# Products of probabilities and values: one key chunk in each of four slots, or two chunks in each of two

## The chip, the cores and the metric

One core of one Trainium2 chip runs the whole program in one launch. The metric is the device time of that core in microseconds. The engines are TensorE (PE, with its weight loads shown apart as PEld), VectorE (DVE), ScalarE (ACT), GpSimd (POOL) and SyncE (SP), which issues the DMAs.

## The reference

A pre-norm transformer layer in float32: batch B = 4, T = 512 tokens, width 512, 32 query heads of width 16 in 8 groups of four, each group sharing one key/value head, and a gated MLP of width 1376. What matters here is the attention in the middle:

```python
q = (x @ Wq) ...; k = (x @ Wk) ...; v = (x @ Wv) ...          # x = layernorm(resid)
q, k = q * cos + rotate_half(q) * sin, k * cos + rotate_half(k) * sin
att = einsum('bhgqd,bhkd->bhgqk', q, k) / sqrt(16), causal mask
probs = softmax(att)
ctx = einsum('bhgqk,bhkd->bhgqd', probs, v)
x = resid + ctx @ Wo;  x = x + mlp(layernorm(x))
```

## The kernel before, in words

The program has two phases, `phase_1` (projections, rotation, attention) and `phase_2` (output projection of all but the first batch, MLP). The change touches phase 1 alone.

Phase 1 runs over the 4 batches. A batch is 32 slots: 8 groups (`g`, one key/value head with its four query heads) by 4 slots (`i`). Each engine walks the same 32 slots with its own list of work (`iteration` of each engine), and semaphores keep them together. Batches 0 to 2 carry, besides their own attention, the preparation of the batch after them (`has_next`); the last batch carries the start of phase 2 (splitting Wo, the first output projection) instead.

In slot `i` of group `g` TensorE goes through four steps `j`. In each:

- `scores(b, g + 2, i, j)` (matmuls at lines 947 and 950) writes query-key scores of the group after next for one head into one of the three PSUM banks `ps_s`; four heads need four banks in slots 0 and 1 (512 and 384 keys wide) and two banks in slots 2 and 3. That is 12 banks for each group, numbered 0 to 11 here. A bank is written again only when VectorE has taken the row maximum of what was there three banks earlier (`row_max`, line 711). The maxima go, split into two parts and transposed by TensorE (line 956), through a DMA into the rows of the queries.
- `scores_t(b, g, i, j)` (line 972) writes the transposed scores, less the maximum, of key chunk `i` into one of three banks `ps_t`. ScalarE turns them into `probs` (line 585), GpSimd zeroes the masked triangle of the chunk (`mask_probs`, lines 517 and 519).
- `weighted_v(b, g, c)` (line 986) multiplies the probabilities of key chunk `c` (512, 384, 256 and 128 query columns for c = 0 to 3) by values that carry a column of ones, into `ps_o`. The four heads write 32 partitions each, and each product of float32 takes two passes, so a chunk is eight matmuls. It waits until GpSimd has masked the chunk. Chunk 0 also waits until ScalarE has copied out `ps_o` of the group before. The last one signals `pv_done`.
- `dense(...)` works at the next batch: units of four pieces in fixed slots (`UNIT_SLOT`): four transposes of x (slots 6, 7, 9, 10), five projections to be rotated (`R`, slots 11, 13, 15, 18, 22), the value projection (`V`, slot 17) and its transpose (`U`, slot 21). All use the one bank `ps_d`, so a unit waits until the unit before it has been read, by VectorE or ScalarE.

Where the products stand is given by `PV_LAG` and `PV_AFTER`: chunk 0 in slot 3 of its own group after step 2, chunk 1 in slot 0 of the next group after step 1, chunk 2 in slot 1 after step 0, chunk 3 in slot 2 after step 1. After the last group of the last batch chunks 1 to 3 follow in one row. ScalarE copies `ps_o` out in slot 2 (`o_evacuate`), before the exponentials of that slot, and SP then stores it (`store_o`).

VectorE in slot `i` takes the row maxima bank by bank, and after each bank one item of `next_work` or `batch_0_work`: for a rotated unit the slot after it holds `rope_cos` (line 694) and `rope_swap` (line 697), four slots after it `rotated_low` (line 702); for a transposed unit `xt_low` (line 683). GpSimd rotates (`rotate`, lines 501 and 503) in the slot after the unit, ahead of the mask of that slot.

Of the kernel before, what the change touches and what calls it, by code (L numbers as in the profile page):

```python
# [27 lines left out]
NKV, GROUP, DH = 8, 4, 16  # L28
F = 1376
TT, KC = T // P, D // P  # L30
# [23 lines left out]


MAX_AFTER = 3
PV_LAG, PV_AFTER = 3, (2, 1, 0, 1)
T_AFTER = 3
PIECE_AFTER = ((1, 1, 2, 3), (1, 3, 3, 3), (1, 1, 2, 3), (3, 3, 3, 3))
STATS_SLOT, MEAN_SLOT, APPLY_SLOT = 1, 3, 4  # L60
# [33 lines left out]
def positive(count):  # L94

    return not isinstance(count, int) or count > 0
# [117 lines left out]
def phase_1(nc, d, to):  # L214
    with ExitStack() as ctx:
# [117 lines left out]
        def _(sp):  # L333
            def load_x(b):
                for t in range(TT):
                    sp.dma_start(x_in[:, t], d["x"][b, P * t:P * (t + 1)]).then_inc(x_loaded[t], DMA)
# [88 lines left out]
            def iteration(b, has_next):  # L425
                if has_next:
                    sp.wait_ge(xn_ready, TT * (b + 1))
                    load_x(b + 1)
                unit0 = UNITS * b + PRE_UNITS
                number = UNIT_NO if has_next else LAST_NO  # L430
                for slot in range(TT * NKV):
                    g, i = slot // TT, slot % TT
                    if i == 0 and g + 3 < NKV:
                        stage_rows(b, g + 3, NKV * b + g + 3)
                    if i == 0 and g + 3 >= NKV and has_next:
                        stage_rows(b + 1, g + 3 - NKV, NKV * b + g + 3)
                    if i == 1 and (has_next or g < NKV - 1):
                        stage_max(g + 1, unit0 + number[slot - 1])
                    if i == PV_LAG - 1 and (g >= 1 or positive(b)):
                        store_o(b, g - 1)  # L440
                    if has_next and UNIT_SLOT.get(slot - LO_AFTER, "-")[0] == "R":
                        store_rotated(b + 1, UNIT_SLOT[slot - LO_AFTER][1])
                    if not positive(b) and i >= 2 and g < 6:
                        copy_raw(2 * g + i - 2)
                    if positive(b) and slot == SUMS_SLOT:
                        load_sums(b - 1)
                    if positive(b) and slot == INVERSE_SLOT + 1:
                        store_inverse(b - 1)
                    if not has_next:
                        prepare_batch_0(slot)  # L450
                if not has_next:
                    store_o(b, NKV - 1)
# [87 lines left out]
        def _(act):  # L540
# [63 lines left out]
            def iteration(b, has_next):  # L604
                unit0 = UNITS * b + PRE_UNITS
                slots, number = (UNIT_SLOT, UNIT_NO) if has_next else (LAST_SLOT, LAST_NO)
                for slot in range(TT * NKV):
                    g, i = slot // TT, slot % TT
# [6 lines left out]
                        v_evacuate(unit0 + number[slot - 1])  # L615
                    if i == 1 and (has_next or g < NKV - 1):
                        max_evacuate(b, g + 1, unit0 + number[slot - 1])
                    if i == PV_LAG - 1 and (g >= 1 or positive(b)):
                        o_evacuate(b, g - 1)
                        if g == 0:  # L620
                            v_place(b, unit0 - UNITS + V_NO)
# [6 lines left out]
                    if not has_next and WO_HI <= slot < WO_HI + KC:  # L628
                        c = slot - WO_HI
                        act.wait_ge(wo_loaded, DMA)  # L630
                        nc.scalar.copy(to.wo[0][:, c], to.wo[1][:, c].bitcast(F32)).then_inc(wo_hi_ready, 1)
                    if not has_next and FFN_HI <= slot < FFN_HI + KC:
                        c = slot - FFN_HI
# [239 lines left out]
        def _(pe):  # L873
# [118 lines left out]
            def iteration(b, has_next):  # L992
                unit0 = UNITS * b + PRE_UNITS
                slots, number = (UNIT_SLOT, UNIT_NO) if has_next else (LAST_SLOT, LAST_NO)
                for slot in range(TT * NKV):
                    g, i = slot // TT, slot % TT
                    kind, k = slots.get(slot, "--")
                    for j in range(GROUP):
                        if has_next or g < NKV - 2:
                            scores(b, g + 2, i, j)  # L1000
                        scores_t(b, g, i, j)
                        before, c = divmod(slot - PV_LAG, TT)
                        if j == PV_AFTER[c] and (before >= 0 or positive(b)):
                            weighted_v(b, before, c)
                        if i == 0 and j == MAX_AFTER and (has_next or g < NKV - 1):
                            transposed_max(NKV * b + g + 1, g + 1, unit0 + number[slot])
                        if kind == "T" and j == T_AFTER:
# [4 lines left out]
                                if PIECE_AFTER[i][piece] == j:  # L1012
                                    dense(b + 1, kind, k, unit0 + number[slot], piece)
                if not has_next:
                    for c in range(TT - PV_LAG, TT):
                        weighted_v(b, NKV - 1, c)

            pe.wait_ge(consts_ready, 1)
# [438 lines left out]
```

## Time and profile before

| | |
|---|---|
| time, median of 3 | 878.38 us (877.71 to 879.62) |
| the profiled execution's own time | 873.69 us |
| its span | 871.9 us |
| PE busy | 823.9 us, 94% |
| DVE, ACT, POOL busy | 54%, 38%, 20% |
| granted TensorE clock over the span | 0.99 |
| start, before the slots | 0 to about 68 us |
| batches 0, 1, 2, 3 of phase 1 | from about 68, 169, 269 and 369 us |
| phase 2 | from about 461 us |

A start in the timeline is in microseconds from the first instruction. The duration that stands with a matmul contains its way through the array, so that successive matmuls overlap; the distance from one start to the next is what it costs. One full-width matmul of 512 columns costs some 0.23 us so, and 0.39 us stand beside it.

### The profile page before, as it was taken

How to read it: one execution, taken by the hardware profiler on the slowest of the kernel's cores; microseconds unless marked ns; L12 is line 12 of the kernel's file. 1: busy time of each engine (PE TensorE's matmuls, PEld its weight loads, DVE VectorE, ACT ScalarE, POOL GpSimd, SP SyncE). 2: the span in 40 equal slices, each digit the busy share in tenths (PEclk: the TensorE clock that was granted, in tenths of full speed). 3: DMA queues.
4: the chain of work that ended last, by engine and by line, in shares of the span. 5: the costliest groups of instructions: out<-in, count | busy, mean ns of one | idle time of the engine just before them, and what ended most of it. 6: DMA issues, size and time to landing. Idle time of an engine off the chain costs nothing. (4 is left out here: it accounts for less than half of the span.)

```text
span 871.9 us, 13600 instructions
## 1 busy us (share of the span) xinstructions
PE 823.9 (94%) x4544; PEld 580.4 (67%) x4544; DVE 471.6 (54%) x861; ACT 332.4 (38%) x659; POOL 177.0 (20%) x349
## 2 busy tenths in 40 slices
PE   1869998999999999999999899999999999999998
PEld 1645665556555666556557688788887888888886
DVE  7569766797778785787753454333333233231112
ACT  2115544675466654675583222211112111121111
POOL 5213344333543253432330000000000000000000
PEclk9969999999999999999999999999999999999999
DMA  5166666631355224464518620041200411020001
GB/s 192 61 190 202 191 194 220 203 93 56 115 165 178 83 78 135 144 193 126 155 37 250 183 72 25 1 156 38 73 25 33 137 56 52 12 77 20 0 1 49
DMA packets 67824, 93.05 MB, mean 107 GB/s; under 512 B 7056, under 2 KB 34704, under 8 KB 67568
## 3 DMA queue, kind: packets, MB, share of 16 engines
q1 hardware_dynamic: 67776, 92.43, 34.1%
q8 instruction: 28, 0.46, 0.2%
q14 instruction: 20, 0.16, 0.1%
HBM read 60.16 MB, written 41.22 MB: 116 GB/s over the span
## 5 line engine op out<-in xcount | busy, mean ns | idle before, releaser
L711 DVE TENSOR_REDUCE m_raw<-ps_s 128x1 f32<-128x384 f32 (+3 forms) x384 | 215.5, 594 | 87.6 <-PE ps_s L950 86.5
L585 ACT ACTIVATE probs<-ps_t 128x512 f32<-128x512 f32 (+2 forms) x384 | 196.0, 529 | 125.3 <-PE ps_t L972 124.4
L947 PE MATMUL ps_s<-k_rows,q_rows 96*128 96x256 f32 (+3 forms) x512 | 166.5, 358 | 16.8 <-DMA k_rows<-scratch_k_parts 11.4
L972 PE MATMUL ps_t<-q_rows,k_rows 98*128 98x512 f32 (+2 forms) x384 | 167.0, 439 | 1.0 <-DMA q_rows<-m_t 0.8
L947 PEld LDWEIGHTS ps_s<-k_rows,q_rows 96*128 96x128 f32 x512 | 95.1, 194 | 89.5 <-issue 39.0
L1278 DVE TENSOR_TENSOR h<-h,bank 128x512 f32<-128x512 f32 (+1 forms) x44 | 30.2, 687 | 220.4 <-PE bank L1321 219.2
L950 PE MATMUL ps_s<-mask_q,ident_b 128*128 128x128 bf16 (+1 forms) x384 | 97.1, 253 | 0.0
L986 PE MATMUL ps_o<-probs,v_ones 128*32 128x512 f32 (+3 forms) x1024 | 95.2, 444 | 0.5 <-POOL probs L519 0.3
L1216 ACT ACTIVATE h<-bank 128x512 f32<-128x512 f32 (+1 forms) x44 | 26.3, 599 | 152.1 <-PE bank L1321 152.1
L519 POOL TENSOR_SCALAR_AFFINE_SELECT probs<-probs 128x512 f32<-128x512 f32 x128 | 81.4, 636 | 0.0
L972 PEld LDWEIGHTS ps_t<-q_rows,k_rows 98*128 98x128 f32 x384 | 76.8, 201 | 6.2 <-ACT probs L585 4.9
L1222 ACT CAST h_hi<-h 128x512 fp32r<-128x512 f32 (+1 forms) x44 | 27.3, 620 | 127.0 <-DVE h L1278 127.0
L950 PEld LDWEIGHTS ps_s<-mask_q,ident_b 128*128 128x128 bf16 x384 | 38.0, 99 | 48.8 <-issue 38.1
L517 POOL TENSOR_TENSOR carrier<-half 128x1 f32<-128x1 f32 x128 | 27.1, 212 | 212.2 <-ACT probs L585 212.2
L1373 PE MATMUL ps_y<-wd_hi,h_hi 128*128 128x512 f32 (+1 forms) x176 | 69.5, 395 | 0.0
L1373 PE MATMUL ps_y<-wd_hi,h_lo 128*128 128x512 f32 (+1 forms) x176 | 69.0, 392 | 0.0
L1373 PE MATMUL ps_y<-wd_lo,h_hi 128*128 128x512 f32 (+1 forms) x176 | 68.6, 390 | 0.0
L195 POOL TENSOR_TENSOR var_eps<-mean_var,eps 128x1 f32<-128x1 f32 x16 | 3.1, 191 | 289.5 <-DVE mean_var L190 289.5
L1321 PE MATMUL bank<-xt_hi,wu_hi 128*128 128x512 f32 (+1 forms) x128 | 50.6, 395 | 0.0
L1321 PE MATMUL bank<-xt_hi,wg_hi 128*128 128x512 f32 (+1 forms) x128 | 50.6, 395 | 0.0
L1321 PE MATMUL bank<-xt_hi,wu_lo 128*128 128x512 f32 (+1 forms) x128 | 50.5, 395 | 0.0
L1321 PE MATMUL bank<-xt_lo,wg_hi 128*128 128x512 f32 (+1 forms) x128 | 50.5, 394 | 0.0
(135 smaller groups left out, 1290.2 us busy)
## 6 DMA issues: line engine op xcount, KB each, us to landing
q_rows<-scratch_q_parts SPq DMA_DIRECT2D x64, 192.0 KB, 3.8
scratch_q_parts<-r_hi SPq DMA_DIRECT2D x32, 256.0 KB
scratch_o<-o_sb SPq DMA_DIRECT2D x31, 256.0 KB, 2.1
k_rows<-scratch_k_parts SPq DMA_DIRECT2D x64, 96.0 KB, 4.1
x_in<-in_x SPq DMA_DIRECT2D x16, 256.0 KB, 4.0
scratch_q_parts<-r_lo SPq DMA_DIRECT2D x16, 256.0 KB
x_res<-in_x SPq DMA_DIRECT2D x16, 256.0 KB, 2.8
o_in<-scratch_o SPq DMA_DIRECT2D x64, 64.0 KB
```

The source lines that it names most:

```text
L517: nc.gpsimd.tensor_tensor(carrier[:, g % 2, c:c + 1], half[:, 0:1], half[:, 0:1], ALU.add)
L519: nc.gpsimd.affine_select(out=diagonal, in_=diagonal, compare_op=ALU.is_ge, fill=0.0, base=0, pattern=[[0, GROUP], [1, P]], channel_multip ...
L585: nc.scalar.activation(probs[:, g % 2, heads * u:heads * (u + 1), CHUNK_AT[c]:CHUNK_AT[c + 1]], ps_t[:, (BANK_AT[c] + u) % S_BANKS, 0:head ...
L711: nc.vector.tensor_reduce(out=m_raw[:, g % 2, at:at + heads], op=ALU.max, axis=AXIS.X, in_=ps_s[:, (BANK_AT[i] + u) % S_BANKS, 0:heads * w ...
L947: nc.tensor.matmul(bank[:, place], q_rows[r][0:PAIR, j, P * q:P * (q + 1)].bitcast(F32R), k_rows[r][0:PAIR, 0:width].bitcast(F32R), start= ...
L950: nc.tensor.matmul(bank[:, :, P * q:width], ident_b[:], mask_q[:, 0:heads, :], start=False, stop=True).then_inc(scores_ready, 1)
L972: nc.tensor.matmul(ps_t[:, (BANK_AT[c] + u) % S_BANKS, 0:heads * width], k_rows[r][:, P * c:P * (c + 1)].bitcast(F32R), q_rows[r][:, heads ...
L986: mm = nc.tensor.matmul(ps_o[32 * j:32 * j + 2 * DH, P * c:T], v_ones[:, c, g % NKV, :], probs[:, g % 2, j, CHUNK_AT[c]:CHUNK_AT[c + 1]], ...
L1222: nc.scalar.copy(h_parts[0][0:m, r], h[0:m, r]).then_inc(h_hi_ready, 1)
L1278: nc.vector.tensor_tensor(h[0:m, r], h[0:m, r], bank[units["up", f] % BANKS][0:m, :], ALU.mult).then_inc(h_ready, 1)
L1321: mm = nc.tensor.matmul(out, weights(w, c), moving(m, c), start=(c == 0 and n == 0), stop=(c == chunks - 1 and n == 2))
L1373: mm = nc.tensor.matmul(ps_y[:, t], h_parts[w][0:m, r, P * t:P * (t + 1)], wd[p][0:m, f, :], start=(f == 0 and k == 0), stop=(f == FT - 1 ...
```

## The change

Chunks 0 and 1 of a group are multiplied together in slot 3 of the group after step 1, chunks 2 and 3 together in slot 1 of the next group after step 1. The slot in which ScalarE copies the result out and SP stores it stays 2 (`PV_EVACUATE` replaces `PV_LAG - 1`). After the last group chunks 2 and 3 follow, instead of 1 to 3. No matmul is added or removed, and no wait inside `weighted_v` is changed.

```diff
-PV_LAG, PV_AFTER = 3, (2, 1, 0, 1)
+PV_SLOT = {1: (-1, (2, 3), 1), 3: (0, (0, 1), 1)}
+PV_EVACUATE = 2
...
-                    if i == PV_LAG - 1 and (g >= 1 or positive(b)):
+                    if i == PV_EVACUATE and (g >= 1 or positive(b)):
                         store_o(b, g - 1)
...
-                    if i == PV_LAG - 1 and (g >= 1 or positive(b)):
+                    if i == PV_EVACUATE and (g >= 1 or positive(b)):
                         o_evacuate(b, g - 1)
...
                         scores_t(b, g, i, j)
-                        before, c = divmod(slot - PV_LAG, TT)
-                        if j == PV_AFTER[c] and (before >= 0 or positive(b)):
-                            weighted_v(b, before, c)
+                        after, chunks, at = PV_SLOT.get(i, (0, (), GROUP))
+                        if j == at and (g + after >= 0 or positive(b)):
+                            for c in chunks:
+                                weighted_v(b, g + after, c)
...
                 if not has_next:
-                    for c in range(TT - PV_LAG, TT):
+                    for c in PV_SLOT[1][1]:
                         weighted_v(b, NKV - 1, c)
```

## Rows read from the trace of the kernel before

**Rows 1.** The page, busy time of each engine: us, share of the span, instructions.
```profile
PE 823.9 (94%) x4544; PEld 580.4 (67%) x4544; DVE 471.6 (54%) x861; ACT 332.4 (38%) x659; POOL 177.0 (20%) x349
```

**Rows 2.** Windows, batches 1 and 3: busy us of each engine, clock, DMA share, GB/s.
```profile
169.00:269.00 100.00, 98.75 (x677) 58.88 (x676) 76.36 (x150) 59.32 (x124) 39.83 (x76) 1.00 0.41 121
...
369.00:460.00 91.00, 87.90 (x618) 49.40 (x617) 65.35 (x124) 61.13 (x130) 29.46 (x75) 1.00 0.41 123
```

**Rows 3.** Timeline of PE, batch 1, slots 12 and 13: start, us, instruction.
```profile
203.98 0.48 PE L972 MATMUL ps_t<-q_rows,k_rows 98*128 98x512 f32 x1
204.30 0.40 PE L947 MATMUL ps_s<-k_rows,q_rows 96*128 96x512 f32 x1
204.54 0.23 PE L950 MATMUL ps_s<-mask_q,ident_b 128*128 128x128 bf16 x1
204.59 0.48 PE L972 MATMUL ps_t<-q_rows,k_rows 98*128 98x512 f32 x1
205.00 0.85 PE L986 MATMUL ps_o<-probs,v_ones 128*32 128x384 f32 x8
205.78 0.50 PE L947 MATMUL ps_s<-k_rows,q_rows 96*128 96x512 f32 x1
206.12 0.23 PE L950 MATMUL ps_s<-mask_q,ident_b 128*128 128x128 bf16 x1
...
207.41 0.42 PE L972 MATMUL ps_t<-q_rows,k_rows 98*128 98x384 f32 x1
207.75 0.64 PE L986 MATMUL ps_o<-probs,v_ones 128*32 128x256 f32 x8
208.32 0.45 PE L947 MATMUL ps_s<-k_rows,q_rows 96*128 96x384 f32 x1
208.61 0.23 PE L950 MATMUL ps_s<-mask_q,ident_b 128*128 128x128 bf16 x1
```

**Rows 4.** Timeline of PE, end of phase 1, two narrow windows.
```profile
458.04 0.72 PE L986 MATMUL ps_o<-probs,v_ones 128*32 128x384 f32 x8
...
458.37 0.61 PE L986 MATMUL ps_o<-probs,v_ones 128*32 128x256 f32 x8
```

**Rows 5.** Timeline of DVE, batch 1, slot 12.
```profile
204.21 0.69 DVE L711 TENSOR_REDUCE m_raw<-ps_s 128x1 f32<-128x512 f32 x1 [2.32 <-PE ps_s L950]
204.82 0.68 DVE L694 TENSOR_TENSOR rot_c<-ps_d,cos 128x512 f32<-128x512 f32 x1
...
206.02 0.73 DVE L697 STREAM_SHUFFLE rot_s<-ps_d 128x512 f32<-128x512 f32 x1
206.65 0.67 DVE L711 TENSOR_REDUCE m_raw<-ps_s 128x1 f32<-128x512 f32 x1
```

**Rows 6.** Timelines of DVE and PE, batch 1, slots 19 and 20.
```profile
235.89 1.78 DVE L702 TENSOR_TENSOR r_lo<-rot_c,r_hi 128x512 fp32r<-128x512 f32 x1
...
238.32 0.51 PE L947 MATMUL ps_s<-k_rows,q_rows 96*128 96x512 f32 x1 [0.84 <-DVE m_raw L711]
```

**Rows 7.** Timelines of POOL and PE, batch 1, slots 23 and 25.
```profile
253.17 0.63 POOL L519 TENSOR_SCALAR_AFFINE_SELECT probs<-probs 128x512 f32<-128x512 f32 x1
...
253.76 0.45 PE L947 MATMUL ps_s<-k_rows,q_rows 96*128 96x384 f32 x1
```

**Rows 8.** Timelines of DVE and PE, batch 1, slot 10.
```profile
197.76 0.68 DVE L683 TENSOR_TENSOR xt_lo<-ps_d,xt_hi 128x512 fp32r<-128x512 f32 x1
...
198.02 0.47 PE L972 MATMUL ps_t<-q_rows,k_rows 98*128 98x512 f32 x1
198.50 0.33 PE L888 MATMUL ps_d<-ident,xn 128*128 128x128 f32 x1
```

**Rows 9.** Timelines of ACT and PE, batch 1, slot 22.
```profile
243.02 0.59 ACT L562 COPY v_next<-ps_d 128x512 f32<-128x512 f32 x1
...
243.66 0.50 PE L899 MATMUL ps_d<-xt_hi,w_hi 128*128 128x512 f32 x1 [0.29 <-ACT v_next L562]
```

**Rows 10.** Waits of PE from 70 to 450 us: total us, times, longest.
```profile
PE ps_s L947 <- DVE m_raw L711: 4.3, 6, 1.4
```

## The prediction, on record before the changed kernel ran

> **What bounds the kernel now.** I read the page first: TensorE is busy 824 of 872 us, every other engine at most 54% [rows 1]. Then the windows by batch: inside a middle batch TensorE has matmuls in flight for 98.75 of 100 us, VectorE for 76, and the clock is full [rows 2]; the reader is to see that phase 1 is bound by TensorE's stream, with VectorE as the only other engine that is near. The list of waits says how near: over some 380 us TensorE waited 4.3 us for VectorE to free a score bank, 6 times [rows 10]. Last the timelines of single slots, which give what a visit to the product of probabilities and values costs, and how much earlier than needed each bank, mask and copy was ready. That last quantity, which I call spare below, decides this case.
>
> **What joining two chunks saves.** Take chunk 1 in [rows 3]. Without a product between them, a transposed-score matmul is followed by the next score matmul after 204.30 - 203.98 = 0.32 us, and that by its mask after 0.24: 0.56. With the product in between the same stretch is 206.12 - 204.59 = 1.53. So the visit costs 0.97 us. Its stream alone: one pass of chunk 1 takes 0.33 us where a pass of chunk 2 follows it (its second pass starts at 458.04, the first pass of chunk 2 at 458.37 [rows 4]), so two passes take 0.65. The rest, 0.33, is the price of a visit: 0.09 on the way in, the remainder at the end and in the next score matmul, which stands with 0.50 instead of 0.40 us. Chunk 2: 208.61 - 207.41 = 1.20 with it; without it a 384-wide pair of distances is about 0.43, so 0.77, of which two thirds of chunk 1's stream, 0.43, and again 0.34. I take 0.33 for all four chunks. That nothing of it is left between two chunks in one row is what [rows 4] show: the second pass of chunk 1 and the first of chunk 2 are 0.33 apart, which is stream alone. The new kernel makes two visits for each group instead of four: 0.65 us less. There are 32 groups; the last had its chunks 1 to 3 in one row already. 31 x 0.65 = 20 us of TensorE time go. That is the upper end of what can be won.
>
> The Trainium skill, TensorEngine Tiling (Array Packing), Key Properties, states that a change of tiling mode drains TensorE; the 0.33 us above agree with a drain on both sides of a 32-column product. The same page, under PSUM Bottleneck, warns that a faster TensorE part may only move the bound to the engines that read PSUM; by that rule nothing of the 20 us need arrive, and the next part works out from rows how much does.
>
> **What the moved products uncover.** No product is gone; they are moved, and where one stood something else was hidden. Call the lead how much earlier than before TensorE reaches a point, counted from the start of the group. In slot 0 of a group the product of chunk 1 (0.97) is gone, in slot 1 the visit of chunk 2 (0.77) comes after bank 5 instead of before bank 5: at bank 5 the lead would be 1.74. Behind it stand chunks 2 and 3 together, then nothing in slot 2, chunks 0 and 1 together in slot 3: from bank 5 to the end of the group the new order is 1.74 - 0.65 = 1.09 us longer than the old. So a group ends at 1.09 minus the lead that it really had at bank 5. With the full lead it wins 0.65; with none it loses 1.09.
>
> The lead is capped by VectorE. Bank 5 needs bank 2 read. A bare reading is spaced at 0.60 us, and TensorE without a product needs 0.32 + 0.24 + 0.04 = 0.60 for each bank too, so any other work of VectorE in slots 0 and 1 shows. Group by group, for a batch with a next one:
>
> - Group 3: VectorE has the cosine product and the swap in slot 12. It works without a gap from 204.21 and ends bank 2 at 206.65 + 0.67 = 207.32 [rows 5]; TensorE started bank 5 at 208.32 [rows 3]. The spare is 1.00, so the lead is 1.00 and not 1.74: +0.1 us. That VectorE's chain here doesn't move with TensorE is seen from its having no gap.
> - Group 4 has the same two operations in slot 16: +0.1, and in slot 18 the projection behind the value unit loses its cover of chunk 3: a further 0.2 (my estimate: less than half of the next such place).
> - Group 5: VectorE's subtraction took 1.78 us instead of the 0.68 of its kind beside a rotation on GpSimd, and TensorE already waited for it at 238.32 [rows 6]. The lead at bank 3 is nil; only chunk 2's 0.77 remains at bank 5: +0.3. In slot 22 the projection waited for ScalarE's copy, ending 243.61, with chunk 3 (0.21 + 0.33 = 0.54) standing before it [rows 9]; chunk 3 is now earlier, the copy isn't: +0.55. Together +0.9.
> - Group 6: chunk 3 of group 5 is masked at 253.80, because two rotations stand before it on GpSimd. It was used in slot 26; now it is wanted in slot 25. TensorE began bank 5 at 253.76 [rows 7]; with a lead of about 1.35 (slot 23's swap delays VectorE a little) it begins at 252.4, and the joined product is due 0.65 later, at 253.05. It waits about 0.8: 1.09 - 1.35 + 0.8 = +0.5. While it waits, scores, transposed scores and the whole TensorE queue stand behind it.
> - Group 2: in slot 10 the transposes need the bank that VectorE empties at 198.44. They came at 198.50, and would have come at 198.02 + 0.32 = 198.34 [rows 8]. Without chunk 3 in front they would come at 197.80: 0.55 more wait. With 0.15 for the same operation in slot 8 the group wins nothing: +0.05.
> - Groups 0, 1 and 7 have spare: group 7 wins 0.6; group 0 0.3 (VectorE starts late over the turn of the loop, my estimate), group 1 0.4 (two normalisations in slot 4).
>
> Sum of a batch: -0.3 - 0.4 + 0.05 + 0.1 + 0.3 + 0.9 + 0.5 - 0.6 = +0.55; three batches +1.7. In the last batch VectorE is as busy (65 of 91 us) [rows 2], with the splitting of Wo and the first contexts in slots 4 to 20; five groups of the kind of group 3 at +0.1 to +0.5 give +1.5, groups 0 and 6 together win 0.6, and at the very end chunk 1's stream, 0.65, now stands before the last transposed scores, whose exponential, mask and product are the chain that closes the phase, and there is nothing else for it to hide behind; some 0.4 for chunk 3's cover in slots 26 and 28. Together +2.0. Sum: +3.7 us.
>
> The other edits cost nothing. ScalarE's copy of the result stays in slot 2 and no longer has to wait there; it is no engine that binds. SP's store follows the copy, so it comes no later. The copy must be done before chunk 0 in slot 3, which is only one step earlier. Chunk 1 is wanted a whole slot earlier than before, but its mask is made in slot 1 and it is used in slot 3. In the last group a wait of TensorE for the last mask is there in both. Phase 2 isn't touched.
>
> The profiled execution took 873.69 us; 873.7 + 3.7 = 877.4. The median of the runs shown is 4.7 above the profiled one, and I carry the difference over: 878.4 + 3.7 = 882.1 us.
>
> **Rivals.**
>
> A. *TensorE alone binds.* All of the 20 us arrive: 858 us. For it speaks the 98.75% in [rows 2]; against it the spare of 1.00 where 1.74 is needed, which is a fact of the rows. 5%.
>
> B. *VectorE's chain slides along (the other side).* The place is banks 2 to 5 of each group. If VectorE, idle for 2 us during the joined product of slot 3, starts each group with its earlier work done, then the caps of groups 0 to 5 shrink, and only the waits for mask, copy and transposes (0.8 + 0.55 + 0.2 + 0.55 = 2.1 a batch, 6.3 in all), group 5's old wait of 0.84 (2.5 in all) and about 2 us in the last batch remain: 20 - 11 = 9 us won, 869 us. It decides from the point where bank 5's real spare is over about 1.1 us in most groups. For it: VectorE sat idle 2.32 us before slot 12 [rows 5]. Against: it was idle there before, and the cap was there all the same. 18%.
>
> C. *The waits stack.* A late bank pushes the reading of the next, and the joined product of 1.9 us in slot 3 delays the swap, the rotation on GpSimd and the mask behind it. Then light groups lose too, 0.2 us more in each of 31: 888 us. 17%.
>
> D. *It comes out even*, the caps a little smaller than counted, within 0.2% of 878.4: 16%.
>
> My forecast, a small loss of 2 to 6 us: 44%.
>
> **How the numbers follow.** About 0.2%, 1.8 us, is what a measurement of this kernel tells from no change. Faster by more: A and B, 23%, and 2% for the mild side of D: 25%. Within: 17%. Slower: the forecast and nearly all of C, 58%. The range holds B and C and leaves A and the far ends out: 868 to 888 us. The forecast's own range is 880 to 885.
>
> **What would show it.** In the profile of the changed kernel the visits of L986 number 64 instead of 126, and the span between the two chunks of one visit holds no gap: this shows the saving. TensorE's waits for L711 should rise from 4.3 us to some 12, with bank 5 of groups 3 and 4 among them; a wait of about 0.8 us for the mask should stand at slot 25, of about 0.9 for the value copy at slot 22, and of about 0.7 for L683 at slot 10. If these waits are absent, B or A is right; if a light group (7) doesn't run about 0.6 us faster, the saving itself is wrong. If the batches take less than 98.5 us each, my caps are too hard.

## The result, and the profile after

The changed kernel is slower: 888.1 us, median of four (885.73 to 888.61), against 878.4 for the kernel before beside it; ratio 1.0107, interval 1.0087 to 1.0127. The direction was forecast, the size was not: +9.7 us where +3.7 were expected, just past the end of the range.

The page first: busy time of each engine, the granted clock in 40 slices, and the group of the products.

```profile
PE 822.1 (93%) x4544; PEld 592.2 (67%) x4544; DVE 467.8 (53%) x861; ACT 332.1 (37%) x659; POOL 177.0 (20%) x349
...
PEclk9967998999999999999999899999999999999999
...
L987 PE MATMUL ps_o<-probs,v_ones 128*32 128x512 f32 (+3 forms) x1024 | 85.5, 450 | 1.5 <-POOL probs L520 0.8
```

Every line number below is one higher than before from this change on (L986 is now L987, L711 is L712). The products went from 95.2 us in flight to 85.5 and TensorE's sum from 823.9 [rows 1] to 822.1, yet the span grew from 871.9 to 886.2. Next TensorE's waits, between 70 and 465 us (total, times, longest):

```profile
PE ps_s L948 <- DVE m_raw L712: 10.7, 14, 1.8
PE ps_d L957 <- DVE rot_s L698: 3.5, 6, 0.6
PE ps_d L889 <- DVE xt_lo L684: 2.9, 4, 1.2
PE ps_d L900 <- ACT v_next L563: 1.9, 3, 0.6
PE ps_t L973 <- ACT probs L586: 0.5, 1, 0.5
```

The first was 4.3 us [rows 10]; L889 and L900 were 0.5 and 0.9 in the kernel before, and the second, the transposed maximum that waits until VectorE has swapped halves out of `ps_d`, was not in the list of before and is not in the forecast either. The first four rows together hold 13.3 us more of waiting than before, against 20 us that the joining saves. By that alone the kernel would be faster.

The windows show what no list of waits does (columns as in [rows 2]; the clock is the number ahead of the last two):

```profile
147.00:245.80 98.80, 93.27 (x651) 58.96 (x650) 73.60 (x146) 57.43 (x120) 39.24 (x74) 1.00 0.44 133
245.90:249.20 3.30, 3.30 (x24) 1.74 (x23) 1.30 (x4) 1.12 (x4) 0.78 (x2) 0.50 0.63 191
249.40:348.20 98.80, 93.18 (x650) 58.75 (x648) 73.29 (x146) 57.64 (x120) 38.49 (x73) 1.00 0.39 116
348.30:351.60 3.30, 3.30 (x21) 1.76 (x23) 2.29 (x4) 1.72 (x4) 1.41 (x4) 0.50 0.54 131
```

Once in each middle batch, in group 5, the granted clock is 0.50, that is 1.2 instead of 2.4 GHz, for some 3.4 us. In batch 0 the same place has it for 6.7 us, from 140.1. What stood before it is in TensorE's timeline of slots 19 and 20 (start, duration, operation):

```profile
238.59 1.71 PE L987 MATMUL ps_o<-probs,v_ones 128*32 128x512 f32 x16
240.23 0.44 PE L948 MATMUL ps_s<-k_rows,q_rows 96*128 96x128 f32 x2
...
244.52 0.50 PE L948 MATMUL ps_s<-k_rows,q_rows 96*128 96x512 f32 x1 [1.81 <-DVE m_raw L712]
...
246.78 1.51 PE L987 MATMUL ps_o<-probs,v_ones 128*32 128x256 f32 x16
```

The same joined product of chunks 2 and 3 took 0.86 us at full clock (in group 7, at 271.37), here 1.51. VectorE in that stretch:

```profile
241.19 0.73 DVE L698 STREAM_SHUFFLE rot_s<-ps_d 128x512 f32<-128x512 f32 x1
242.10 1.76 DVE L703 TENSOR_TENSOR r_lo<-rot_c,r_hi 128x512 fp32r<-128x512 f32 x1
```

Lastly the lengths of the groups, from the start of one group's first transposed scores to that of the next, batch 1, worked out from the timelines (batch 2 agrees within 0.02 us in both kernels, but for group 0 of the changed one, which takes 9.77 there):

```
group       0      1      2      3      4      5      6      7
before    9.98  11.32  13.72  15.39  15.46  14.59   9.89   9.89
after     9.46  11.67  13.83  15.57  15.99  16.97  10.13   9.28
           -0.52  +0.35  +0.11  +0.18  +0.53  +2.37  +0.24  -0.60   (from unrounded starts)
forecast   -0.3   -0.4  +0.05   +0.1   +0.3   +0.9   +0.5   -0.6
```

### The profile page after: what moved, and what is told of

Its sections match the earlier page's. It is cut to its first block and busy times, and to the rows that moved or that the text cites. A ratio compares the mean times of both kernels' runs of the same rounds, so it can differ in the third digit from the quotient of the medians.

```text
span 886.2 us, 13600 instructions
## 1 busy us (share of the span) xinstructions
PE 822.1 (93%) x4544; PEld 592.2 (67%) x4544; DVE 467.8 (53%) x861; ACT 332.1 (37%) x659; POOL 177.0 (20%) x349
## 5 line engine op out<-in xcount | busy, mean ns | idle before, releaser
L712 DVE TENSOR_REDUCE m_raw<-ps_s 128x1 f32<-128x384 f32 (+3 forms) x384 | 214.1, 594 | 107.7 <-PE ps_s L951 106.2
L948 PE MATMUL ps_s<-k_rows,q_rows 96*128 96x256 f32 (+3 forms) x512 | 161.4, 357 | 21.7 <-DVE m_raw L712 10.7
L973 PE MATMUL ps_t<-q_rows,k_rows 98*128 98x512 f32 (+2 forms) x384 | 171.6, 451 | 3.2 <-DMA q_rows<-m_t 2.6
L948 PEld LDWEIGHTS ps_s<-k_rows,q_rows 96*128 96x128 f32 x512 | 97.9, 200 | 59.9 <-DVE m_raw L712 24.7
L951 PE MATMUL ps_s<-mask_q,ident_b 128*128 128x128 bf16 (+1 forms) x384 | 98.9, 258 | 0.0
L987 PE MATMUL ps_o<-probs,v_ones 128*32 128x512 f32 (+3 forms) x1024 | 85.5, 450 | 1.5 <-POOL probs L520 0.8
L973 PEld LDWEIGHTS ps_t<-q_rows,k_rows 98*128 98x128 f32 x384 | 79.6, 208 | 7.5 <-ACT probs L586 3.7
L987 PEld LDWEIGHTS ps_o<-probs,v_ones 128*32 128x32 f32 x1024 | 27.3, 112 | 39.3 <-issue 23.8
```

What stands on the lines that cost most here:

```text
L712: nc.vector.tensor_reduce(out=m_raw[:, g % 2, at:at + heads], op=ALU.max, axis=AXIS.X, in_=ps_s[:, (BANK_AT[i] + u) % S_BANKS, 0:heads * w ...
L948: nc.tensor.matmul(bank[:, place], q_rows[r][0:PAIR, j, P * q:P * (q + 1)].bitcast(F32R), k_rows[r][0:PAIR, 0:width].bitcast(F32R), start= ...
L951: nc.tensor.matmul(bank[:, :, P * q:width], ident_b[:], mask_q[:, 0:heads, :], start=False, stop=True).then_inc(scores_ready, 1)
L973: nc.tensor.matmul(ps_t[:, (BANK_AT[c] + u) % S_BANKS, 0:heads * width], k_rows[r][:, P * c:P * (c + 1)].bitcast(F32R), q_rows[r][:, heads ...
L987: mm = nc.tensor.matmul(ps_o[32 * j:32 * j + 2 * DH, P * c:T], v_ones[:, c, g % NKV, :], probs[:, g % 2, j, CHUNK_AT[c]:CHUNK_AT[c + 1]], ...
```

## The experiments

Three theories. **T1, the caps:** the joining saves its 0.65 a group and the readers of PSUM on VectorE and ScalarE take it back, as forecast. **T2, the clock:** a wait behind which the granted clock falls costs more than its own length. **T3, the order:** it is not the joining but which chunk is moved out of which slot.

**The kernel before, once more** (`r_before`, unchanged).

> The kernel before once more, for a second profile of it. Its first profile took 873.7 us at a mean clock of 0.990, while 17 other executions of it stood at 0.970 to 0.978 and 876.6 to 882.5 us. Theory: the first profile was an execution in which the clock stayed full at the start of the slots; this one shows 876 to 880 us, with group 0 of batch 0 some 4 to 5 us longer at half clock and all groups of batches 1 and 2 as in the first. Rival: the 5 us lie elsewhere, in the middle groups or the second phase.

879.08 us, ratio 0.9996. Its profile is not like the first one of before:

```profile
44.00:78.00 34.00, 29.15 (x107) 19.34 (x107) 24.53 (x49) 9.06 (x18) 3.93 (x9) 0.50 0.68 212
78.20:463.00 384.80, 375.62 (x2579) 221.56 (x2576) 284.61 (x548) 232.06 (x487) 145.27 (x293) 1.00 0.45 137
```

Here the clock is 1.2 GHz for the 34 us in which the slots begin, and group 0 of batch 0 takes 13.08 us; in the first profiled execution it is full from 60.6 us and that group takes 8.38. This is not the whole difference of the two profiles: the slots begin 2.4 us earlier in the second, group 1 of batch 0 is 0.9 shorter, and phase 2 is 2.6 longer, with two more stretches at half clock, one of them this:

```profile
463.80:467.10 3.30, 3.30 (x9) 2.52 (x9) 1.19 (x2) 0.66 (x2) 0.00 (x0) 0.50 0.77 248
```

Together the span is 4.0 us longer. Batches 1 and 2 agree group by group within 0.01 us, and the clock there is full. So this profile (span 875.9) is the one to compare with: after is 10.3 longer, 8.3 of it in phase 1 (404.91 against 396.63), 1.35 ahead of the slots, 0.7 in phase 2. Of the 8.3, group 5 of three batches is 7.6 (2.88, 2.37, 2.38). In batch 0 that group took 15.57 before and not 14.60, because TensorE also waited 0.71 us there for the DMA of `k_rows`, which it doesn't in the changed kernel.

**Which join** (T3). Chunks 0 and 1 joined and the others alone; chunks 2 and 3 joined and the others where they were. (The chunks that follow after the last group are adapted in each of these kernels; the cuts leave that line out.)

```diff
 # e1_join01
+PV_SLOT = {1: (-1, (2,), 0), 2: (-1, (3,), 1), 3: (0, (0, 1), 1)}
 # e2_join23
+PV_SLOT = {0: (-1, (1,), 1), 1: (-1, (2, 3), 1), 3: (0, (0,), 2)}
```

> Half of the change: chunks 0 and 1 together in slot 3, chunks 2 and 3 left where they were. Theory 1 (covers and clock): one visit less for each group is worth 0.33 us, 10 us in all; chunk 1 no longer covers slot 0, so the wait of TensorE for VectorE in slot 20 grows from 1.0 to about 2.0 us in each of three batches, as in the changed kernel, and the granted clock falls to half behind it for some 3.4 us; the waits at slot 10, 22 and 25 don't appear. Sum -10 + 3 (slot 20) + 3 (other capped groups) + 4 (clock) = about 878 us, 874 to 884. Rival (only the covers count, the clock falls for reasons of its own): 874 us and the same stretches at half clock as in the changed kernel's first group. Rival 2 (a visit costs nothing to join): slower than before by the waits alone, 884 or more.

> The other half: chunks 2 and 3 together in slot 1, chunks 0 and 1 left where they were. Theory 1: -10 us for the visits; slot 20's wait stays at 1.0 us because chunk 1 still covers slot 0, so the clock doesn't fall in the middle batches; the waits at slot 10 (0.7), slot 22 (0.9) and a small one at slot 25 appear, +1.5 us a batch. About 873 us, 869 to 878. Rival (the clock falls wherever waits add up, also from slots 10, 22 and 25): 880 us or more with half-clock stretches in groups 5 and 6.

`e1_join01` 892.5 us, 1.0137 (1.0099 to 1.0175): a miss of 14 us. It has the loss of the change and more: group 5 takes 18.0 to 19.5 us with 7 to 10 us at half clock, groups 3 and 4 lose 0.5 each. `e2_join23` 876.2 us, 0.9973 (0.9951 to 0.9995): group 5 takes 14.78, the clock doesn't fall in the middle batches, the light groups win 0.3 to 0.4. So the join of chunks 2 and 3 alone is slightly good, by 0.27%, and inside the 869 to 878 expected. The loss came with the other, which takes chunk 1's product out of slot 0, from before the bank that VectorE frees late.

**Both pairs joined, but a slot later** (T3): chunk 1 back in slot 0, with chunk 0.

```diff
 # e3_later
+PV_SLOT = {0: (-1, (0, 1), 1), 2: (-1, (2, 3), 1)}
+PV_EVACUATE = 3
```

> The same joining, but the pairs stand later instead of earlier: chunks 0 and 1 together in slot 0 of the next group after step 1, chunks 2 and 3 together in slot 2 after step 1, result copied out in slot 3. So slots 0 and 2 keep their cover. Theory 1: all of the 0.65 us for each group arrive, the wait in slot 20 shrinks to nothing, no wait at slots 10, 22, 25, clock full: 856 to 864 us. Rival (VectorE's total work caps phase 1 wherever the products stand): no more than 5 us below before, 873 or more. Rival 2 (a long product burst by itself makes the score banks or the exponentials late): waits of TensorE for VectorE or ScalarE above 10 us, 875 us or more.

886.3 us, 1.0080 (1.0054 to 1.0105): a miss. Where it was aimed it hit, group 5 is 0.74 shorter than before and group 6 0.62 in batch 1, with a full clock there. The gain went elsewhere. TensorE's waits, same columns and stretch as above:

```profile
PE ps_s L948 <- DMA k_rows<-scratch_k_parts: 3.6, 3, 2.6
PE ps_s L948 <- DVE m_raw L712: 3.4, 10, 0.5
PE ps_d L889 <- DVE xt_lo L684: 3.2, 4, 1.2
PE ps_d L900 <- DVE xt_lo L684: 2.1, 3, 0.7
PE ps_t L973 <- DMA q_rows<-m_t: 1.9, 2, 1.6
```

Group 1 lost 0.88, and in the last batch the last two groups lost 3.5 (four chunks now stand at the tail) and the first two 1.6 against the first profile of before, 1.0 against the second. So this order uncovers other things; which product had covered which was not taken apart.

**Is it the subtraction?** VectorE's L703 stands before bank 3 of group 5 and took 1.76 us. In one kernel it works on one column of 512 for that unit, in the other zeros are written in its place; neither computes the low part of that unit.

```diff
 # e4_no_low2
+                width = 1 if k == 2 else T
-                nc.vector.tensor_tensor(r_lo[:, r], rot_c[:, r], r_hi[:, r].bitcast(F32),
+                nc.vector.tensor_tensor(r_lo[:, r, 0:width], rot_c[:, r, 0:width], ...
 # e5_zero2
+                if k == 2:
+                    nc.vector.memset(r_lo[:, r].bitcast(F32), 0.0).then_inc(r_lo_ready, 1)
+                    return
```

> The changed kernel with one piece of VectorE's work left out: the subtraction of rotated unit 2, in slot 19, is done on 1 column instead of 512 (the low part of those queries is then not computed). Theory 1: the wait of 1.8 us in slot 20 falls to about 0.3, and as that wait is what lets the clock fall in group 5, the half-clock stretches of batches 1 and 2 go too: three times 1.6 + 1.4 = 9 us less than the changed kernel's 888, 879 us, group 5 of batch 1 about 14 us instead of 16.97. Rival (the clock falls for reasons of its own, with the start of the run): only three times 1.6, 883 us, group 5 at 15.4 us with the clock still halved there.

> The changed kernel, with the subtraction of rotated unit 2 in slot 19 replaced by writing zeros (the low part of those queries is left out). One column of that subtraction still took 1.23 us in e4, because it stood behind GpSimd's rotation, which reads two tensors; a write of zeros reads nothing. Theory 1 (the lock with GpSimd makes the wait of slot 20, and that wait lets the clock fall): zeros take about 0.5 us and don't wait for GpSimd; TensorE's wait in slot 20 falls from 1.8 to under 0.8, the half-clock stretches of batches 1 and 2 in group 5 are gone, group 5 takes 14.3 to 14.8 us instead of 16.97, and the median is 6 to 8 us below the changed kernel's 888: 880 to 882. Rival (the waits of slots 21, 22 and 25 are enough to make it fall): group 5 still above 16 us, 883 to 885. Rival 2 (no lock; VectorE is late because of its own amount of work): zeros take over 1 us as well, nothing moves.

`e4_no_low2`: 889.0 us, no better, and the miss is the finding. (Its profiled execution took 880.0; group 0 of batch 0, 9.03 us there and about 13 in most profiles, holds some 4 of the 9.) Timelines of VectorE, GpSimd and TensorE:

```profile
235.35 1.23 DVE L704 TENSOR_TENSOR r_lo<-rot_c,r_hi 128x1 fp32r<-128x1 f32 x1
...
235.25 1.31 POOL L502 TENSOR_TENSOR rot_s<-rot_s,sin 128x512 f32<-128x512 f32 x1 [2.97 <-DVE rot_s L698]
...
237.24 0.49 PE L949 MATMUL ps_s<-k_rows,q_rows 96*128 96x512 f32 x1 [1.28 <-DVE m_raw L713]
```

One column took 1.23 us and ended at 236.58, when the first half of GpSimd's rotation had ended (236.56). So most of it isn't work. The rotation is a product (L502) and a sum (L504), each of two tensors in SBUF. The wait of 1.28 us that is left again stands before a stretch at half clock:

```profile
238.90:242.20 3.30, 3.30 (x24) 1.62 (x24) 1.54 (x4) 0.94 (x3) 0.68 (x2) 0.50 0.60 181
```

`e5_zero2`: a write with no input isn't held. VectorE's row, and the window over the place that fell in the others:

```profile
242.54 0.48 DVE L704 MEMSET r_lo<- 128x512 f32 x1
```
```profile
240.00:249.00 9.00, 7.87 (x61) 4.67 (x53) 6.80 (x16) 5.60 (x13) 4.85 (x8) 1.00 0.32 82
```

TensorE's wait is 0.62, the clock is full in group 5, which takes 14.48, 14.25 and 14.28 us, as expected; the time is 881.5, 1.0024 (0.9993 to 1.0055). Against 16.97 that is 2.7 us for each middle batch, of which 1.2 is the shorter wait (1.81 to 0.62). The other 1.5 goes with the stretch of 3.3 us at half clock; `q_after`, below, gives the same price inside one kernel. The Trainium skill, SBUF — State Buffer, Who interferes with whom, states that a VectorE operation with two SBUF inputs and a GpSimd operation that reads SBUF block one another whole; the 1.23 us for a single column agree.

**Half of the change by order, the other half without its block** (T3). Chunks 2 and 3 joined in slot 2; then the same place cured by turning two items of VectorE, so that the subtraction runs at the head of its slot, ahead of GpSimd's rotation, in both kernels and in both good variants.

```diff
 # e6_join23_late
+PV_SLOT = {0: (-1, (1,), 1), 2: (-1, (2, 3), 1), 3: (0, (0,), 2)}
 # f_before, f_after, f_join23 (on e2), f_e6 (on e6): the turned item
-                    work.append(lambda: rotated_low(b + 1, split))
+                    work.insert(0, lambda: rotated_low(b + 1, split))
```

> Chunks 0 and 1 where they were before, chunks 2 and 3 together in slot 2 after step 1, where chunk 3 was. Slot 2 keeps its cover, slot 0 too; only slot 1 loses chunk 2's. Theory 1: the wait for x low at slot 10, for ScalarE's copy at slot 22 and for the mask at slot 25 are as before or smaller, the lead at bank 5 is 0.77 where the spare was 1.0, so all of the 0.33 us for each of 31 groups arrives: 10 us less, 867 to 871, no half clock in the middle batches. Rival (bank 5 or the transposed maximum is capped as soon as any cover leaves): 875 to 878.

> The changed kernel with one item of VectorE's order turned: in a slot that holds the subtraction of a rotated unit and the cosine product and swap of another (slot 19), the subtraction comes first, before GpSimd can start its rotation. Everything is computed. Theory 1 (lock with GpSimd, then the wait of slot 20, then the clock): the subtraction takes 0.7 us instead of 1.8, the wait of slot 20 falls under 1 us, group 5 takes 14.3 to 15 us instead of 16.97 with the clock full, and the median is about 882 us, as with the zeros (881.5). Rival (the subtraction now waits for ScalarE's high part, or the later swap delays the rotation and the masks as much as was won): group 5 above 16 us, 886 or more.

> The kernel before with the same turned item. The wait of 0.84 to 1.0 us in slot 20 goes in three batches: 3 us less, about 876 us, clock no different. Rival: nothing, because the wait is covered by chunk 1 standing before it.

> Chunks 2 and 3 together in slot 1 (e2, 876.2 us), with the same turned item. If both gains are independent: 876.2 - 3 = 873 us, better than the kernel before, the changed one and e2. Rival: the wait for ScalarE's copy in slot 22 or the mask in slot 25 takes it back, 876.

> Chunks 2 and 3 together in slot 2 (e6, 879.3), with the turned item. Group 5 without the wait of slot 20. If the two add up: 876; if e6's loss lay in a late VectorE in the last batch, which the turned item doesn't touch, the same 876, and then the joining in slot 1 (f_join23, 874.2) stays the better one. Below 873 would say that covers in slot 2 are worth more than the one in slot 1.

```
kernel           us      ratio (interval)           group 5, batch 1
e6_join23_late   879.3   1.0017 (0.9991 - 1.0042)   14.02
f_after          885.7   1.0062 (1.0028 - 1.0095)    14.96
f_before         875.0   0.9945 (0.9918 - 0.9972)    13.51
f_join23         874.2   0.9947 (0.9929 - 0.9964)    14.27
f_e6             873.5   0.9948 (0.9917 - 0.9978)    12.93
```

Turned, the subtraction takes its own time and TensorE's wait at that bank shrinks (rows of VectorE and TensorE, `f_after`):

```profile
239.60 0.68 DVE L703 TENSOR_TENSOR r_lo<-rot_c,r_hi 128x512 fp32r<-128x512 f32 x1
...
244.11 0.50 PE L948 MATMUL ps_s<-k_rows,q_rows 96*128 96x512 f32 x1 [0.73 <-DVE m_raw L712]
```

Group 5 of the changed kernel falls from 16.97 to 14.96, with a full clock there. But `f_after` (about 882 expected, a miss) has falls elsewhere. One is in group 1 of batch 1, right after two short waits for row maxima:

```profile
184.64 0.45 PE L948 MATMUL ps_s<-k_rows,q_rows 96*128 96x384 f32 x1 [0.70 <-DVE m_raw L712]
185.70 0.44 PE L948 MATMUL ps_s<-k_rows,q_rows 96*128 96x384 f32 x1 [0.31 <-DVE m_raw L712]
...
186.10:192.80 6.70, 6.70 (x37) 4.55 (x36) 4.48 (x9) 2.98 (x6) 0.78 (x2) 0.50 0.10 37
```

It costs 3.1 us (group 1 takes 14.75 us there and 11.66 in batch 2); a second one of 3.4 us, in group 3 of the last batch, costs 1.5. `e5_zero2` has the first one too, from 186; the changed kernel itself, with the same waits, does not. Turning helps the kernel before (-4 us of median, 3 expected) at least as much as the changed one, so the block is an old loss that the change enlarged, not the whole of its loss: `f_after` stays 10.7 us above `f_before`. `e6_join23_late` (867 to 871 expected, a miss) wins 1.5 us in each middle batch and gives 2.1 back in the last, where TensorE waits 2.3 for VectorE; turned, it has the lowest median of the kernels that compute everything, but its interval and those of the other two lie on one another. The wait of 2.3 us bears on T2, for the clock did not fall behind it:

```profile
425.13 0.51 PE L948 MATMUL ps_s<-k_rows,q_rows 96*128 96x256 f32 x2 [2.34 <-DVE m_raw L712]
...
425.10:435.00 9.90, 9.49 (x69) 5.34 (x70) 9.58 (x19) 7.11 (x15) 3.04 (x8) 1.00 0.12 41
```

**The caps** (T1). In the pair `q_before` and `q_after` each row maximum is taken over the first 64 keys of a bank only, and the exponential is scaled by a thousandth so that no sum runs over: VectorE's readings are short, everything else keeps its place. In `n_after`, built on `f_after`, the normalisation of batches 1 to 3 works on 8 of 512 columns, which frees VectorE in slots 4 and 5.

```diff
 # q_before, q_after
-                        ACT.Exp, scale=SCALE).then_inc(exp_done, 1)
+                        ACT.Exp, scale=SCALE * 1e-3).then_inc(exp_done, 1)
...
-                        in_=ps_s[...].rearrange("p (j t) -> p j t", j=heads)
+                        in_=ps_s[...].rearrange("p (j t) -> p j t", j=heads)[:, :, 0:64]
 # n_after
+                width = D if isinstance(b, int) and b == 0 else 8
+                nc.vector.tensor_scalar(xn[:, t, 0:width], x_in[:, t, 0:width], ...
```

> The kernel before, with the row maximum taken over the first 64 keys of each bank only, so that VectorE's reading of a bank is short (some 0.2 us instead of 0.6), and the exponent scaled by 0.001 so that the exponentials stay finite; probabilities are not the reference's. It is the base for the next one. Theory: TensorE's waits for VectorE (4.3 us) mostly go: 870 to 876.

> The changed kernel with the same short row maximum. Theory 1 (the cap by VectorE's reading eats the saving): with the cap gone the groups with a short chain win their 0.65 us against q_before; groups 5 and 6 still pay for the value copy, the mask and the locked subtraction. Group 3 and 4 turn from +0.2 and +0.5 to below -0.2 each, phase 1 is 5 to 12 us shorter than q_before's. Rival (joined products cost the same as single ones, the light groups' -0.6 had another cause): no difference between the two or q_after slower.

> The changed kernel with the turned item (f_after, 885.7), and the normalisation of x for batches 1 to 3 done on 8 of 512 columns (the rest of the normalised x is left as it was, so the later batches are computed from wrong values). That takes some 1.7 us of VectorE's work out of slots 4 and 5. Theory 1: the waits of 0.96 and 0.47 us in slots 4 and 5 go, group 1 takes about 10.2 to 10.5 us instead of 11.7 (or 14.8 with the clock halved) and has the clock full; 877 to 880 us. Rival (the fall in group 1 comes at a fixed time of the run and not from waits): a half-clock stretch near 186 us stays, 882 or more.

`q_before` 875.0 us, `q_after` 868.2: without the cap the same change wins 6.8 us. By groups of batch 1, `q_after` less `q_before`:

```
-0.72  -0.66  -0.24  -0.63  -0.28  +2.43  +0.11  -0.60
```

Groups 0, 1, 3 and 7 win the 0.65 that was worked out, within 0.1. Group 5 keeps its loss, because the block of the subtraction is still there (a wait of 1.26 us and a stretch at half clock). In batch 2 the wait is 1.22, the clock holds, and the group is +0.86: 14.85 us against 16.42. So a stretch of 3.3 us at half clock cost 1.57 in one and the same kernel. The windows show that stretch in batch 1, and the whole of group 5 in batch 2:

```profile
236.50:239.70 3.20, 3.20 (x23) 1.85 (x24) 0.25 (x2) 0.96 (x3) 0.46 (x1) 0.50 0.63 184
...
330.00:345.00 15.00, 13.13 (x92) 8.36 (x91) 6.87 (x21) 7.81 (x17) 5.96 (x10) 1.00 0.46 139
```

`n_after` is at 878.4, 0.9989 (0.9963 to 1.0016), 7 us below `f_after`; group 1 takes 11.14 (expected 10.2 to 10.5: half a hit), one wait of 0.44 is left there of the two, and no middle batch has a fall. In the profiles some 3 of these 7 us are the fall of `f_after` in that group.

**The clock by itself** (T2). The kernel before, every product where it was, with a write to a scratch tensor put on VectorE at the end of slot 19, before the bank for which TensorE waits already: 512 columns once, or 1536.

```diff
 # w1_small_wait; w2_long_wait with 1536 columns
+        pad = sb("pad", [P, T])
...
+                if slot == 19:
+                    for _ in range(1):
+                        work.append(lambda: nc.vector.memset(pad[:], 0.0))
```

> The kernel before with one write of zeros (512 columns, to a tile that nobody reads) added on VectorE at the end of slot 19, ahead of the reading of bank 0. TensorE's wait in slot 20 grows from 0.84 by about 0.4, to 1.2 to 1.3 us. Theory 1 (a wait of such size lets the clock fall, whatever the order of the products): e4 had 1.28 and the clock fell in every batch, q_after had about as much and it fell in one of two; so it falls in some: group 5 at 15.0 us where the clock stays, at 16.5 where it falls; median 880 to 885. Rival (the long joined product is what makes the clock fall): group 5 at 15.0 in all batches, 880.5.

> The same with 1536 columns, some 1 us: TensorE's wait in slot 20 becomes about 1.8 to 2 us, as in the changed kernel, with every product where it was before. Theory 1: the clock falls to half in group 5 of each of the three batches, group 5 takes 17 to 18 us instead of 14.6, of which 1.0 to 1.2 is the wait itself; 886 to 889 us. Rival (joined products needed): group 5 at 15.7, 882.5 us.

`w1_small_wait` 885.9 us, 1.0070 (1.0039 to 1.0101). The wait is 1.32 in all three batches, 0.48 more than before. After it the clock fell in batches 0 and 1 and held in batch 2; TensorE's row in batch 1, and the two windows:

```profile
245.82 0.58 PE L951 MATMUL ps_s<-k_rows,q_rows 96*128 96x512 f32 x1 [1.32 <-DVE m_raw L712]
...
246.10:252.90 6.80, 6.80 (x29) 4.23 (x29) 3.69 (x7) 2.73 (x7) 1.22 (x3) 0.50 0.65 185
...
253.00:348.00 95.00, 94.88 (x648) 56.21 (x647) 71.97 (x141) 56.20 (x117) 36.86 (x72) 1.00 0.39 114
```

Group 5 takes 17.71, 17.82 and 15.09 us. So one program shows both: with the clock held a wait longer by 0.48 costs 0.49, with a fall 3.2. `w2_long_wait` 894.6 us, 1.0177 (1.0119 to 1.0236), more than the 886 to 889 expected:

```profile
246.02 0.51 PE L951 MATMUL ps_s<-k_rows,q_rows 96*128 96x512 f32 x1 [2.38 <-DVE m_raw L712]
...
247.60:254.30 6.70, 6.70 (x34) 4.18 (x27) 3.58 (x7) 3.24 (x8) 1.55 (x4) 0.50 0.57 171
```

1.54 us more of waiting, the clock fell in all three, and group 5 takes 18.91, 18.83 and 20.07 against 14.6: 4.2 to 5.5 more. So 2.7 to 3.9 us of each are the clock's, for stretches of 6.7 to 10.2 us. That such a wait can bring the clock down, and what that costs, is shown with no product moved; which waits do so is not (see Open).

## Why the prediction was right or wrong

**What joining saves: right.** The visits are 64 instead of 126, the joined product has no gap where no mask is late (group 6 is the exception), group 7 runs 0.60 faster (forecast 0.6), and without VectorE's cap four groups win 0.60 to 0.72.

**The lead is capped by VectorE: right in kind.** Without the cap 6.8 us are won, with it 9.7 are lost. Groups 0, 2, 3, 4 and 7 came within 0.25 of the forecast. Group 1 is off by 0.75: two normalisations on VectorE leave no lead at bank 4, where I had claimed spare without a row for it. That `n_after` shortens group 1 by 0.53 and leaves one wait of 0.44 where there were two, 0.70 and 0.31, bears this out. For groups 3 and 4 I missed a cap of the same size one step earlier: the transposed maximum needs `ps_d` empty, six waits of some 0.6. Group 3 came out at +0.18 even so; the further 0.35 of group 4 (+0.53 instead of +0.3) are in slot 18, where the projection lost its cover, an estimate of 0.2. The waits for L712 did rise, to 10.7 where some 12 were named, but bank 5 of groups 3 and 4 of a middle batch is not among them. The last batch was forecast at +2.0 and gave -0.3 (sum of its eight groups; -0.65 against the second profile of before): its list of work for VectorE is full, but group 4 there won 1.47, because a wait of 1.41 us for VectorE became 0.52, which I hadn't looked for. That this miss and the one of group 1 (2.1 us over three batches) nearly cancel is luck.

**Waits named ahead: two of three.** TensorE's rows at slot 22, then those at slot 10:

```profile
250.43 0.48 PE L973 MATMUL ps_t<-q_rows,k_rows 98*128 98x512 f32 x1
251.56 0.50 PE L900 MATMUL ps_d<-xt_hi,w_hi 128*128 128x512 f32 x1 [0.64 <-ACT v_next L563]
```
```profile
202.27 0.47 PE L973 MATMUL ps_t<-q_rows,k_rows 98*128 98x512 f32 x1
203.29 0.55 PE L889 MATMUL ps_d<-ident,xn 128*128 128x128 f32 x3 [0.55 <-DVE xt_lo L684]
```

Against the bare distance of 0.32 slot 10 loses 0.70 (forecast 0.7), slot 22 0.81 (forecast 0.9). The mask at slot 25 was forecast at 0.8 and cost 0.3:

```profile
261.68 1.19 PE L987 MATMUL ps_o<-probs,v_ones 128*32 128x256 f32 x16
262.79 0.44 PE L948 MATMUL ps_s<-k_rows,q_rows 96*128 96x384 f32 x1
...
271.37 0.86 PE L987 MATMUL ps_o<-probs,v_ones 128*32 128x256 f32 x16
272.16 0.44 PE L948 MATMUL ps_s<-k_rows,q_rows 96*128 96x384 f32 x1
```

From start to start that is 1.11, and of the same pair one group later 0.79: the joined product runs chunk 2 first, and only chunk 3 needs the late mask. I had let the whole joined product wait; in group 6 that gives +0.24 instead of +0.5.

**Where it failed: group 5, +0.9 forecast, +2.4 measured, three times, and the clock.** The step reads "the lead at bank 3 is nil; only chunk 2's 0.77 remains": it counts the length of the wait rightly and gives it no second price. With chunk 1's product gone from slot 0, TensorE comes to the bank 0.97 sooner. VectorE doesn't, because its subtraction stands behind GpSimd, so the wait of 0.84 [rows 6] became 1.81, longer by 0.97, exactly the visit. The sum of lead and spare holds this: without the 1.5 us of the clock (`e5_zero2`, `q_after`) group 5 would be +0.9, as forecast. What the sum did not have is what the clock takes behind such a wait. "The clock is full" was read from [rows 2] and carried over to a kernel whose longest wait there is twice as long.

The stretch at half clock costs 1.5 us in each middle batch. In batch 0, where it lasts 6.7 us, it costs 3.0: 18.45 us against the 15.5 that the group takes without it (16.97 less 1.5). That is 6.0 in all. From the forecast's +3.7 to the measured +8.3 of phase 1 the parts are these: 6.0 for the clock, 2.1 for group 1 of three batches, 2.65 less in the last batch, and 1.0 less in batch 0, where the wait for the DMA is gone; what is left of the other groups is about 0.2. Without the clock phase 1 would be at +2.3, so the forecast's 3.7 was near it only by misses that cancel. The 1.35 us ahead of the slots lies in the start, where the two executions of before differ by 2.4, and I claim no cause for it.

**The 4.7 us between profile and median** were carried over as a plain sum. That did no harm: the changed kernel's own profiled execution (887.9) lies at its median. The 4.70 that group 0 of batch 0 takes more in `r_before` equal the gap by chance, since other parts of the two profiles differ by up to 2.6 us both ways. What is shown is that the clock differs between executions of one kernel, at the start of the slots and in phase 2.

**The 0.33 us of a visit** are measured. That they are a drain of TensorE, as the prediction reads them, is not shown: the transposed maximum is a 32-column matmul too, and it stands only 0.03 us from its neighbour (last section).

**The rivals.** A fell: the unhindered gain isn't there. B fell: in no group except in the q pair does VectorE slide along. C's time was the nearest (888), and not for its reason: the light groups 0 and 7 win more than 0.5 each, and the largest part of the loss sits in one group. No rival had the clock.

**Open.** Which waits let the clock fall isn't settled, and their length alone doesn't decide it. After 1.28 us it fell in three batches of three (`e4_no_low2`), after 1.32 in two of three, after some 1.25 in one of three (`q_after`), and after 0.70 and 0.31 in one batch of `f_after` and of `e5_zero2`, but not in the changed kernel. It did not fall after 0.84 in any profiled execution of before, nor in the last batch of before after 1.41 and 1.25, nor in `e6_join23_late` after 2.34. What stood before each such stretch is in the rows, the rule isn't.

The listed waits don't close the sum either. The joining saves 20; against it stand 13.3 listed, 2.6 for 17 more waits at whose start the list leaves out some 0.15 each (0.70 against 0.55 at slot 10), 1 for the mask and 6.0 for the clock, and the DMA's wait of 1.0 is gone. That is a loss of 2, and phase 1 lost 8.3. Steps too short for the list hold 2.2 of the rest, three times 0.35 in slot 18 and three times 0.39 at bank 2 of group 6, and the last waits of phase 1 another 1.0. For some 3 us I have no row.

Versions faster than both exist: `f_before`, `f_join23` and `f_e6` are 0.5% below before, each with its interval below 1. The turned item alone gives it; joining chunks 2 and 3 beside it lowers the median by a further 0.9 to 1.5 us, which isn't told from nothing.

## What to carry to other kernels

Before a stream of work is tidied, read what each piece covers: a product that stands between a bank and its slow reader is paid for already, and moving it away saves its switch and uncovers the reader. Price a new wait on TensorE of about a microsecond twice: its length, and some four tenths of any stretch that then runs at 1.2 GHz (here 1.5 us of 3.3, 2.7 to 3.1 of 6.7). No list of waits shows such a stretch; windows over the time behind the wait do. And look first for the root of an existing wait: turning one item on VectorE was worth more than the rearrangement.

## What the runs showed of the hardware

- TensorE's granted clock halved behind single waits of 1.3 to 2.4 us in a stream that was otherwise matmul on matmul, for 3.3 to 10.2 us at a time, and not every time: it held behind 1.32 us in one batch of `w1_small_wait` and behind 2.34 us in `e6_join23_late`.
- A stretch of 3.3 us at half clock cost 1.57 us between two batches of `q_after`; one of 6.7 us cost 2.7 between two batches of `w1_small_wait` and 3.1 between two of `f_after`.
- A VectorE subtraction of one column took 1.23 us beside a two-tensor operation on GpSimd; of 512 columns 1.76 beside it and 0.68 away from it. A write of 512 columns without input took 0.48 in the same place.
- A visit of a 32-column product between full-width ones cost 0.33 us beyond its stream; a single 32-column transpose (L956) stands 0.03 from its neighbour:

```profile
239.03 0.27 PE L956 MATMUL ps_d<-ident,m_parts 128*32 128x128 f32 x1
239.06 0.42 PE L947 MATMUL ps_s<-k_rows,q_rows 96*128 96x384 f32 x1
```

- Two profiled executions of the kernel before differ in the clock where the slots begin: the first group took 13.08 us in the one and 8.38 in the other.
